# Mixture of experts in a four-layer kernel: routing weights and bias applied behind the down products, GpSimd adds up the experts, spreads of half the width

## The reference

```python
logits = xf @ gate_w + gate_b
probs = jax.nn.softmax(logits, axis=-1)
top2_vals, top2_idx = jax.lax.top_k(probs, 2)
cw = jnp.zeros((N, Ee), dtype=xf.dtype).at[jnp.arange(N)[:, None], top2_idx].add(top2_vals)

def step(acc, params):
    w1, bb1, w2, bb2, we = params
    h = jax.nn.gelu(xf @ w1 + bb1, approximate=False)
    y = h @ w2 + bb2
    return (acc + we[:, None] * y, None)
out, _ = jax.lax.scan(step, jnp.zeros_like(xf), (W1, b1, W2, b2, cw.T))
```

## Time and profile before

| | us |
|---|---|
| median of 3 runs | 422.7 |
| lowest and highest of them | 421.83, 422.84 |
| the profiled execution, own time | 422.28 |
| its span | 420.4 |
| PE busy | 292.6 |
| DVE busy | 257.7 |
| ACT busy | 212.3 |
| POOL busy | 12.1 |

### The profile page before, as it was taken

The page is one execution under the profiler, slowest core; times in us unless marked ns, Lnnn a source line. Parts: engine busy times, 40 slices in busy tenths (PEclk is TensorE's granted clock), DMA queues, the critical chain, the costliest instruction groups (busy, mean ns, idle before and its releaser), DMA issues.

```text
span 420.4 us, 11844 instructions
## 1 busy us (share of the span) xinstructions
PE 292.6 (70%) x3273; PEld 224.5 (53%) x3278; DVE 257.7 (61%) x2308; ACT 212.3 (50%) x1172; POOL 12.1 (3%) x22
## 2 busy tenths in 40 slices
PE   6899889989875666666556666665566666656663
PEld 2466347743455555555555555555555555555553
DVE  1786454655356666666666666666666666666665
ACT  2687253254455555555555555555555555555552
POOL 5410000000000000000000000000000000000000
PEclk9999999799975555555555555555555555555555
DMA  7500000000000000000000000000000000000000
GB/s 278 229 3 2 0 2 1 0 2 0 0 3 2 0 0 0 0 0 0 0 0 0 0 0 0 0 0 0 0 0 0 0 0 0 0 0 0 0 0 12
DMA packets 2972, 5.60 MB, mean 13 GB/s; under 512 B 1424, under 2 KB 1680, under 8 KB 2960
## 3 DMA queue, kind: packets, MB, share of 16 engines
q1 hardware_dynamic: 2672, 5.09, 3.3%
q10 hardware_dynamic: 288, 0.36, 0.2%
HBM read 5.32 MB, written 0.13 MB: 13 GB/s over the span
## 4 chain that ended last, share of the span: by engine, by line
ACT 38%; PE 37%; DVE 14%; issue 9%; DMA 1%; SPq 0%; DVEq 0%
ACT bank L383 20%; PE bank L665 17%; ACT gi L371 10%; DVE ha L949 6%; DVE terms_a L949 4%; ACT bank L373 4%; PE bank L424 2%; PE bank L446 2%; PE bank L394 2%; PE bank L435 1%; PE bank L597 1%; PE bank L558 1%; PE bank L609 1%; DMA cst<-in_const 1%; PE bank L479 1%
## 5 line engine op out<-in xcount | busy, mean ns | idle before, releaser
L665 PE MATMUL bank<-ha,vparts 128*128 128x1 f16 x1536 | 96.0, 169 | 110.8 <-DVE ha L949 110.8
L665 PEld LDWEIGHTS bank<-ha,vparts 128*128 128x128 f16 x1536 | 75.1, 107 | 133.7 <-DVE ha L949 133.7
L371 ACT ACTIVATE gi<-bank 128x1 f32<-128x1 f32 x256 | 43.8, 171 | 145.4 <-PE bank L665 145.4
L383 ACT ACTIVATE bank<-bank,hc,gi 128x2 f32<-128x2 f32 x256 | 83.5, 326 | 0.0
L946 DVE TENSOR_SCALAR go<-go 128x1 f32<-128x1 f32 x256 | 39.4, 154 | 66.3 <-ACT go L377 66.3
L665 PE MATMUL bank<-hb,vparts 128*128 128x1 f16 x768 | 76.4, 165 | 0.0
L665 PEld LDWEIGHTS bank<-hb,vparts 128*128 128x128 f16 x768 | 60.7, 104 | 0.0
L949 DVE CUSTOM_DVE_ANT_0 terms_a<-bank,go 128x3 f32<-128x3 f32 x256 | 41.2, 161 | 29.2 <-ACT bank L383 0.2
L661 PE MATMUL bank<-x,w5s 128*128 (+1 forms) x198 | 56.0, 358 | 0.1
L474 PE MATMUL bank<-ones,w5s 128*128 128x8 f32 x198 | 55.6, 355 | 0.0
L955 DVE SCALAR_TENSOR_TENSOR cell<-bank,gi,hc 128x1 f32<-128x1 f32 x256 | 54.7, 214 | 0.0
(11 more groups left out here) (215 smaller groups left out, 293.6 us busy)
## 6 DMA issues: line engine op xcount, KB each, us to landing
rel<-in_positions SPq DMA_DIRECT2D x4, 352.0 KB, 5.4
w3s<-in_w SPq DMA_DIRECT2D x1, 804.0 KB, 9.6
ltr<-in_later SPq DMA_DIRECT2D x1, 709.0 KB, 7.3
w2s<-in_w SPq DMA_DIRECT2D x1, 640.0 KB, 8.4
w5s<-in_w SPq DMA_DIRECT2D x1, 576.0 KB, 10.6
w0s<-in_w ACTq DMA_DIRECT2D x1, 336.0 KB, 4.0
w1s<-in_w SPq DMA_DIRECT2D x1, 256.0 KB, 7.5
w4s<-in_w SPq DMA_DIRECT2D x1, 192.0 KB, 10.5
```

Of the source, the lines that this page charges most:

```text
L371: act.activation(gi[:], bank[pre + 1][:, at:at + 1], ACT.Sigmoid, scale=1.0 / PRE)
L383: act.activation(tc_ends, gt.broadcast_to([P, 2]), ACT.Tanh, scale=gi[:], bias=hc[:]).then_inc(on("tanh_c"), 1)
L665: return mm(bank[3 * parity + k][:, at:at + 1], vparts[:, part, k], h, start=False, stop=False, skip_group_check=True)
```

## The change

1. Mixture of experts. `down` now reads `hg` as it comes from the gelu, without weights, and every pair of experts has a PSUM bank half each in one of four banks. `spread_weights(k)` spreads the weights of experts 2k and 2k+1 with 256 columns each (the two batches now stand in the rows of `cwt`, 48 rows in place of 24), and ACT copies each pair to the tile `spread`. DVE then computes, for each expert, (down + b2) times weight in one operation, `ye[e]`, 128 x 256. POOL adds `t2` and `ye[0]` to `ye[5]` one after the other into `t3part`; DVE adds `ye[6]` and `ye[7]`. The product with `cwf`, its copy on ACT and the transposes of the unsplit weights are gone.
2. Norms. `rsw` and its copy are gone; PE takes `rs` itself, read 64 times, as the stationary operand, and the identity as the moving one: four float32 products of 64 x 128 in place of two transposes. One `keep_clock` product is taken out ahead of `squares` in norms 1 to 4, and one ahead of `rs` in all five.
3. The table with the exponential is asked for on ACT right behind the root of the group norm.

```diff
@@ POOL
+            pool.wait_ge(on("t2"), 1)
+            for e in range(E - 2):
+                pool.wait_ge(on("weighted"), e + 1)
+                if e:
+                    pool.wait_ge(on("t3_part"), e)
+                pool.tensor_tensor(t3part[:, e], t3part[:, e - 1] if e else t2[:], ye[:, e], ALU.add)\
+                    .then_inc(on("t3_part"), 1)
@@ ACT
             act.activation(gtm[:, 2:3], gtm[:, 1:2], ACT.Sqrt, scale=-1.0, bias=epsc[:, 1:2]).then_inc(on("gsd"), 1)
+            ask_table(ACT.Exp)
...
-            act.wait_ge(on("cw_turned"), 1)
-            act.activation(cwf[:], bank[4][0:E, 0:B * N], ACT.Copy).then_inc(on("cwf"), 1)
...
+            def spread_copy(k):
+                act.wait_ge(on("cw_mm"), k + 1)
+                act.activation(spread[:, 2 * k:2 * k + 2].rearrange("p e n -> p (e n)"), spread_bank[k % 2][:],
+                               ACT.Copy).then_inc(on("spread"), 1)
+
+            for e in range(E - 1):
+                gelu(e)
+            spread_copy(0)
+            gelu(E - 1)
+            for k in range(1, E // 2):
+                spread_copy(k)
@@ PE, norm
-                if n < 5:
-                    keep_clock(rs_bank[n], 1)
-                else:
-
+                if n == 5:
                     b_part(0, 0)
...
-                keep_clock(rs_bank[n], 3)
+                keep_clock(rs_bank[n], 2)
                 pe.wait_ge(on("rs"), n)
                 for h in range(HALVES):
-                    m = pe.transpose(rs_bank[n][:, h * P:(h + 1) * P], rsw[:, h].rearrange("p b c -> p (b c)"), ident)
+                    for b in range(B):
+                        m = mm(rs_bank[n][b * C:(b + 1) * C, h * P:(h + 1) * P], rs[:, h, b:b + 1].broadcast_to([P, C]),
+                               ident, start=True, stop=True)
@@ PE, mixture of experts
+            def spread_weights(k):
+
+                if k == 1:
+                    pe.wait_ge(on("gelu"), 6)
+                if k >= 2:
+                    pe.wait_ge(on("spread"), k - 1)
+                for e in (2 * k, 2 * k + 1):
+                    m = mm(spread_bank[k % 2][:, e % 2 * N:(e % 2 + 1) * N], oneh[:, e * P:(e + 1) * P], cwt[:],
+                           start=True, stop=True)
+                m.then_inc(on("cw_mm"), 1)
 
             def down(e):
-                pe.wait_ge(on("weighted"), e + 1)
+                pe.wait_ge(on("gelu"), e + 1)
...
-            for e in range(UP_FIRST):
+            for e in range(3):
                 up(e)
+            for e in range(3):
+                up(e + 3)
+                down(e)
...
+            up(6)
+            down(3)
             pe.wait_ge(on("cwt"), 1)
             pe.wait_ge(on("oneh_ready"), 1)
...
+            spread_weights(0)
+            up(7)
+            down(4)
+            for k in range(1, E // 2):
+                spread_weights(k)
+                down(k + 4)
             pe.wait_ge(on("t3"), 1)
             norm(4, t3[:])
@@ DVE
                 dve.wait_ge(on("root"), n)
-                link(dve.reciprocal(rs[:], sd[:]))
-                dve.tensor_copy(rsw[:], rs[:][:, :, :, None].broadcast_to([P, HALVES, B, C])).then_inc(on("rs"), 1)
+                dve.reciprocal(rs[:], sd[:]).then_inc(on("rs"), 1)
...
             for e in range(E):
-                dve.wait_ge(on("gelu"), e + 1)
-                dve.wait_ge(on("cw_mm"), e + 1)
-                if e >= 3:
-                    dve.wait_ge(on("down_mm"), e - 2)
-                tt(hw[:, e % 3], hg[:, e], weight_bank[e % 3][:], ALU.mult).then_inc(on("weighted"), 1)
-            dve.wait_ge(on("down_mm"), E)
-            tt(t3[:], bank[7][:, 0:N], t2[:], ALU.add).then_inc(on("t3"), 1)
+                if e % 2 == 0:
+                    dve.wait_ge(on("down_mm"), e + 2)
+                    dve.wait_ge(on("spread"), e // 2 + 1)
+                if e == E - 1:
+                    dve.wait_ge(on("t3_part"), E - 2)
+                    dve.wait_ge(on("weighted"), E - 1)
+                    tt(t3part[:, E - 2], t3part[:, E - 3], ye[:, E - 2], ALU.add).then_inc(on("t3_most"), 1)
+                stt(out=ye[:, e], in0=down_bank[e // 2][:, e % 2 * N:(e % 2 + 1) * N], scalar=v(f"b2_{e}"),
+                    in1=spread[:, e], op0=ALU.add, op1=ALU.mult).then_inc(on("weighted"), 1)
+            dve.wait_ge(on("weighted"), E)
+            dve.wait_ge(on("t3_most"), 1)
+            tt(t3[:], t3part[:, E - 2], ye[:, E - 1], ALU.add).then_inc(on("t3"), 1)
             norm(4, x4[:], "x4")
```

More of the change, by code:

```diff
@@ L51 @@
 W2 = {f"{n}{d}": P for d in range(3) for n in "qkv"} | dict(proj=P)
-W3 = dict(gate=E, b2=C, up=E * HID, down=E * C)
+W3 = dict(gate=E, up=E * HID, down=E * C)
 W4 = dict(fc=P, s0=P, s1=P)
@@ L55 @@
 VEC = ["bq0", "bk0", "bv0_0", "bv0_1", "bp0", "g1b", "g2b", "lng", "lnb", "gamma", "beta", "bq1", "bk1", "bv1", "bp1",
-       "bp2", "fcb"] + [f"b1_{e}" for e in range(E)]
+       "bp2", "fcb"] + [f"b1_{e}" for e in range(E)] + [f"b2_{e}" for e in range(E)]
 VECS = {n: 1 for n in VEC} | dict(gateb=E)
@@ L126, in build @@
         sd, rs = sb("sd", [P, HALVES, B]), sb("rs", [P, HALVES, B])
-        rsw = sb("rsw", [P, HALVES, B, C])
         epsc = sb("epsc", [P, 2])
@@ L161, in build @@
         idb = sb("idb", [P, P], BF16)
-        oneh = sb("oneh", [3 * E, E * P], BF16)
-        cwt = sb("cwt", [3 * E, B * N], BF16)
-        cwf = sb("cwf", [E, B * N])
+        PARTS = B * 3 * E
+        oneh = sb("oneh", [PARTS, E * P], BF16)
+        cwt = sb("cwt", [PARTS, N], BF16)
         hg = sb("hg", [P, E, B * N])
-        hw = sb("hw", [P, 3, B * N])
+        spread = sb("spread", [P, E, N])
+        ye = sb("ye", [P, E, N])
+        t3part = sb("t3part", [P, E, N])
         t3 = sb("t3", [P, N])
@@ L191, in build @@
         dif_bank, var_bank, rs_bank = ({n: bank[3 * (n == 5) + i] for n in range(1, 6)} for i in (0, 1, 2))
-        up_bank, weight_bank = (bank[0], bank[1], bank[5]), (bank[2], bank[3], bank[6])
+        up_bank, down_bank, spread_bank = (bank[0], bank[1], bank[5]), (bank[3], bank[4], bank[6], bank[7]), (bank[2], bank[5])
         v2_bank = (bank[6], bank[7], bank[0])
@@ L232, in _ @@
             pool.wait_ge(on("later_in"), 16)
-            pool.tensor_copy(oneh[:], c("onehot")[0:3 * E]).then_inc(on("oneh_ready"), 1)
+            pool.tensor_copy(oneh[:], c("onehot")[0:PARTS]).then_inc(on("oneh_ready"), 1)
             pool.wait_ge(on("w5_in"), 16)
@@ L348, in _, with gelu @@
             act.activation(eg[:], lg2[:], ACT.Exp).then_inc(on("eg"), 1)
-            for e in range(E):
+            def gelu(e):
                 act.wait_ge(on("up_mm"), e + 1)
                 act.activation(hg[:, e], up_bank[e % 3][:], ACT.Gelu, bias=v(f"b1_{e}")).then_inc(on("gelu"), 1)
-            act.wait_ge(on("cw_turned"), 1)
-            act.activation(cwf[:], bank[4][0:E, 0:B * N], ACT.Copy).then_inc(on("cwf"), 1)
+            def spread_copy(k):
[8 more added lines that the diff above has]
+                spread_copy(k)
             root(4)
@@ L598, in up @@
                    start=True, stop=True).then_inc(on("up_mm"), 1)
-            def spread_weight(e):
-                if e >= 3:
-                    pe.wait_ge(on("weighted"), e - 2)
-                mm(weight_bank[e % 3][:], oneh[:, e * P:(e + 1) * P], cwt[:], start=True, stop=True).then_inc(on("cw_mm"), 1)
+            def spread_weights(k):
[7 more added lines that the diff above has]
+                m.then_inc(on("cw_mm"), 1)
@@ L606, in down @@
             def down(e):
-                pe.wait_ge(on("weighted"), e + 1)
+                pe.wait_ge(on("gelu"), e + 1)
                 for b in range(B):
-                    m = mm(bank[7][b * C:(b + 1) * C, 0:N], cols(w3s, W3, "down")[:, e * C:(e + 1) * C],
-                           hw[:, e % 3, b * N:(b + 1) * N], start=(e == 0), stop=False, skip_group_check=True)
+                    m = mm(down_bank[e // 2][b * C:(b + 1) * C, e % 2 * N:(e % 2 + 1) * N],
+                           cols(w3s, W3, "down")[:, e * C:(e + 1) * C], hg[:, e, b * N:(b + 1) * N],
+                           start=True, stop=True, skip_group_check=True)
@@ L611, in down @@
                 m.then_inc(on("down_mm"), 1)
-            for e in range(UP_FIRST):
+            for e in range(3):
                 up(e)
+            for e in range(3):
+                up(e + 3)
+                down(e)
             pe.wait_ge(on("cw_parts"), 3)
             pe.wait_ge(on("idb_ready"), 1)
-            cwb = bank[3][:].bitcast(BF16)
+            cwb = bank[7][:].bitcast(BF16)
             for h in range(HALVES):
[L619 to L622, removed]
+                m = pe.transpose(cwb[0:PARTS, h * P:(h + 1) * P],
+                                 cwp[:, h * B:(h + 1) * B].rearrange("p b a e -> p (b a e)"), idb[:])
@@ L623, in _ @@
             m.then_inc(on("cw_turned"), 1)
-            up(UP_FIRST)
+            up(6)
+            down(3)
             pe.wait_ge(on("cwt"), 1)
             pe.wait_ge(on("oneh_ready"), 1)
```

(19 more changed lines are left out.)

## The result

The change made the kernel slower: 423.82 us median against 421.9 us (14 runs of each), 1.9 us more. The ratio, which compares the means, is 1.0052 with a 95% interval of 1.004 to 1.0065, that is 2.2 us and at the edges 1.7 to 2.7. The profiled execution of the changed kernel took 423.51 us with a span of 421.7, against 422.28 and 420.4.

A forecast was written before the change was run, and what follows sets the result against it. No engine but the order of a chain bounds the first 118 us; the recurrence is untouched. Table -0.42, norms -0.44 and experts +0.2 give -0.7 us: 421.6 against the profiled 422.28, 422.0 against the 422.7 median; range 420.5 to 424.4.

The forecast's parts named there:

- How the numbers follow: Part of the prediction giving chances: 0.27 faster by over 0.3%, 0.21 slower by over 0.3%, 0.52 within.
- rival B: Behind the experts, PE's queue is empty 3 us and TensorE's clock falls before norm 4 is through: 424.3 us, chance 0.22.
- The rival's price: From norm 4 to norm 5, products at the lower clock: +1.5 to +3.1 us, taken as +2.3 over the sum.
- The experts: Mixture of experts: the 2.4 us that PE saves end in POOL's chain of additions, a cost of +0.2 us.
- POOL's link: In the experts' chain of additions, one POOL addition to the next: 0.70 us, with 0.61 for the addition by proportion.
- rival D: In the experts, POOL pays more for additions beside DVE's work: +1.35 us, 423.1 us; chance 0.13 together with rival E.
- PE's part: In the experts, PE takes 11.5 us from the fourth up to the last down and is done 2.4 us earlier.
- The norms: PE starts 0.33 us earlier without the copy, longer passes give 0.22 back: -0.11 us in each of norms 1 to 4.
- Norm 5: Last norm, where bias products of the recurrence stand in PE's queue: change taken at 0.
- The table: Second layer: of the 1.28 us table load 0.42 us is gained, as the exponential then waits for DVE's minimum.
- rival E: The exponential's table is loaded again because copies between need another one: 422.4 us; chance 0.13 together with rival D.
- The sum without the clock: All three edits with the clock staying full: -0.42 (table), -0.44 (norms), +0.2 (experts), -0.7 us in all.

The follow-up runs named there:

- the run with 14 products: The changed kernel with 14 products of zeros on PE between the last down product and norm 4: 421.3 us, ratio 0.9984 to the kernel before.
- the run with 9 products: The changed kernel with 9 products of zeros on PE between the last down product and norm 4: 421.64 us, ratio 1.0 to the kernel before.
- The run with the delay: The kernel before with six unused, dependent DVE additions between the last down product and t3: 426.92 us, ratio 1.0115.
- the norms and the table alone: The kernel before with only the changes to the norms and the exponential's table, mixture of experts as before: 420.71 us, ratio 0.9967.
- the table alone: The kernel before with only the exponential's table asked for behind the group norm's root: 421.09 us, ratio 0.998.
- the run with the additions on DVE: The changed kernel with all eight additions on DVE, none on POOL, no added products of zeros: 423.44 us, ratio 1.0033 to the kernel before.
- the experts alone: The kernel before with only the new mixture of experts, norms and table as before: 424.25 us, ratio 1.006.
- 5 products of zeros: The changed kernel with 5 products of zeros on PE behind the last down product: 423.81 us, ratio 1.0031 to the kernel before.

## Why the prediction was wrong

**The step that failed** stands in "How the numbers follow": I gave the forecast to the case in which the clock stays full and 0.22 to rival B. The rival's mechanism and place were as written: PE done early, 3 us of empty queue (3.62 in the trace), the lower level from just ahead of norm 4 (105.7) until behind it (112.5). What I held against it, that norm 4's own products come right behind, is refuted: in the changed kernel the clock had fallen 0.4 us before norm 4 began. 13 of 14 executions lay over 423 us. I had no row of an empty PE queue of 3 us and took the lack of a row for a low chance; the rows that I had pointed the other way, since PE lost the clock while busy with narrow products.

The rival's price, +2.3 us, met the +2.34 of the trace (2.25 against the run with 14 products) by luck. The working had six products of 256 columns and the norm's passes on the chain, +3.1 if all fell into a low stretch of 6.8 us, and took a value in the middle. The stretch was 6.8 us long, but only two of the six products fell into it (1.22 in place of 0.70, 0.85 in place of 0.68), and what the working had not at all is the rest. The chain of norm 4 in the changed kernel:

```profile
108.84 0.87 PE bank L415 x2
109.71 1.05 PE bank L515 x8
110.76 0.97 PE bank L415 x2
111.73 0.85 PE bank L667 x2
```

and in the run with 9 products:

```profile
108.01 0.27 ACT sd L323
...
108.30 0.19 DVE rs L796
...
108.53 0.66 PE bank L515 x8
109.19 0.54 PE bank L415 x2
109.73 0.68 PE bank L668 x2
```

L415 is `keep_clock`, and the first product behind the norm is L667 in one program and L668 in the other. At the lower level the norm's own products of zeros last longer than the steps of ACT and DVE that they are to fill, and stand in front of the real ones: 2.5 us of norm 4's chain lie on them in place of 1.0, of 5.6 us in place of 3.5. What fewer of them would give at that level was not tried.

The Trainium skill (TensorE: Matmul & The Clock Gate, The HAM clock gate) has the lower rate as the default of an idle engine. The run with the delay agrees: 3.28 us without work, and the granted clock went from 1.00 to 0.50.

**The experts** came out at +0.57 us in place of +0.2. The term that was mis-sized is POOL's link. Its rows in the changed kernel:

```profile
100.40 0.72 POOL L254 TENSOR_TENSOR t3part<-t3part,ye 128x256 f32<-128x256 f32 x1
101.41 3.34 POOL L254 TENSOR_TENSOR t3part<-t3part,ye 128x256 f32<-128x256 f32 x4 [0.28 <-DVE ye L940]
```

One addition takes 0.72, where proportion from 384 columns gave 0.61, and four take 3.34: (3.34 - 0.73) / 3 = 0.87 from start to start, where I had 0.70. From the first of these four to DVE's L939 it is 3.37 us in place of 2.8. That is POOL's own price and not rival D's: the six additions take 0.723 to 0.733 us, beside DVE's work and while DVE waits for the last one. Proportion failed because the time doesn't go by width alone: by the two rows, 0.72 at 256 columns and 0.91 at 384, an estimate of the part that doesn't depend on width is 0.34 us, if the two operations cost the same otherwise. PE's part was right: from the first of the last five `up` (91.10) to the last `down` through at 102.4 is 11.3 us, where the sum had 11.5.

**The norms** were right to 0.01 us in each of norms 1 to 3: -0.10 against -0.11. Norm 3 in the changed kernel, beside the earlier trace rows of norm 2 before:

```profile
85.19 0.18 DVE L795 RECIPROCAL rs<-sd 128x4 f32<-128x4 f32 x1 [0.53 <-ACT sd L323]
...
85.42 0.66 PE L515 MATMUL bank<-cst,rs 128*64 128x128 f32 x8
...
86.13 0.87 DVE L803 TENSOR_TENSOR x<-dif,bank 64x256 f32<-64x256 f32 x2 [0.76 <-PE bank L515]
```

PE starts 0.23 behind the reciprocal and DVE 0.71 behind PE; the estimates were 0.23 and 0.70. Norm 4, at full clock in the run with 14 products, took 3.54 against 3.63. Norm 5, taken at 0, costs 0.18: products of zeros keep PE until 0.49 behind the reciprocal's start (115.18 in the run with 14 products), 0.07 earlier than with the copy, and the longer passes give 0.23 back.

**The table** gained 0.41 us against the 0.42 of the sum, and the minimum is what the exponential waits for. The table isn't loaded a second time in between, so rival E falls:

```profile
50.91 1.28 ACT L264 ACT_TABLE_LOAD   x1
...
54.61 1.52 DVE L833 TENSOR_REDUCE nm<-bank 128x1 f32<-128x256 f32 x4 [1.21 <-PE bank L541]
...
55.07 0.47 ACT L339 ACTIVATE p<-bank,nm 128x256 f32<-128x256 f32 x1 [0.89 <-DVE nm L833]
```

**The sum without the clock** was -0.7 us. Stage by stage the traces give -0.41 for the table, -0.30 for norms 1 to 3, -0.09 for norm 4, +0.18 for norm 5 and +0.57 for the experts, which is -0.05. The run with 14 products came out at 421.3 us against 421.86, 0.3 to 1.05 us less by the ratio's interval. That looks like the forecast, and it is luck as far as the traces go: of its gain only these 0.05 us lie in stages that the change touches. The same holds for the norms and the table alone (0.6 us in the stages, 0.9 to 1.9 by the ratio) and the table alone (0.4 and 0.5 to 1.2); the cause of the difference stays open.

## What to carry to other kernels

An edit that relieves one engine moves its work ahead and leaves a hole behind it; on TensorE a hole has a price of its own, paid by whatever comes after, so ask of each saving how long PE will have nothing to do and put products of zeros into it, or better, work. Where the clock falls all the same, products of zeros further on lengthen the chain themselves. A chain of small additions on GpSimd costs more per link than width alone says (0.87 us for 256 columns here): count start to start between dependent instructions, and cut links by adding pairs elsewhere. Where a rival is worked out with place and price and only a row is missing for its condition, don't give it a small chance for that; look at the single executions of a changed kernel too, since a median can hide that a stretch goes two ways.

## What the runs showed of the hardware beyond what was expected

The granted clock seems to go two ways in the same program: with 2.42 us of empty queue 8 of 12 executions were over 423 us, with 1.57 us 2 of 12. Nor did it fall at a fixed time after PE's last product: 1.3 us behind it in the run with the additions on DVE, 1.6 in the experts alone, 2.0 with 5 products of zeros, 3.2 in the changed kernel and in the kernel before with a delay.

The clock also goes with the length of the third layer, which changes from execution to execution with the same instructions. The chain at its start and at norm 3, in the changed kernel:

```profile
65.36 0.68 PE bank L571 x2
...
83.08 0.70 PE bank L500 x2
```

and with 14 products of zeros behind the experts, which are no part of this layer:

```profile
66.03 0.68 PE bank L571 x2
...
82.62 0.70 PE bank L500 x2
```

17.7 against 16.6 us. The stretch of 76 to 78 in the first and in the second:

```profile
76.00:78.00 2.00, 2.00 (x10) 1.80 (x9) 0.95 (x3) 1.23 (x2) 0.00 (x0) 0.50 0.00 0
```

```profile
76.00:78.00 2.00, 2.00 (x14) 1.39 (x13) 1.22 (x4) 1.22 (x2) 0.00 (x0) 0.91 0.00 0
```

Of the 14 profiled executions of this study, six gave 16.6 (among them the experts alone and the table alone) and eight 17.6 to 18.1 (among them both kernels, and the norms with the table). Added up from stretches of half a microsecond, the clock is at the lower level for 3.4 us of this layer in each of the six and for 6.8 us in each of the eight, without an exception; what decides between the two is not shown. Differences of a microsecond between two single traces of this kernel are therefore no evidence of an edit unless they lie in its own stage.
